# Summing five neighbours in a local attention: one strided reduction or three contiguous additions on VectorE

## The chip, the cores and the metric

One core of a Trainium2 chip. The metric is the device time of one execution of the whole program in microseconds (us), taken over several executions. The kernel is one launch of hand-placed instructions with semaphores between the engines: PE (matmul), DVE (VectorE), ACT (ScalarE), POOL (GpSimd) and SP, whose queue issues nearly all DMAs.

## The reference

The program is a network of three blocks on x of 8 x 128 x 32 x 32, that is eight images of 1024 tokens with 128 channels. What matters here is the middle block. Cut to that:

```python
def _L1_attn_ref(x, ...):                      # per image, 1024 tokens of 128 channels
    x_global = global_mha(x, ..., H_GLOBAL=8)  # full softmax attention
    x_local = local_mha(x, ..., H_LOCAL=4)     # each token and its 5 neighbours
    x_comb = jnp.concatenate([x_global, x_local], axis=-1)
    ...                                        # fused MLP, layer norm, feed-forward, layer norm

def local_mha(x, ...):
    k_win = jnp.stack([kp[:, j:j + Sq] for j in range(WINDOW)], axis=2)
    v_win = jnp.stack([vp[:, j:j + Sq] for j in range(WINDOW)], axis=2)
    scores = jnp.einsum('bshd,bswhd->bshw', q, k_win) / np.sqrt(hd)
    attn = jax.nn.softmax(scores, axis=-1)
    o = jnp.einsum('bshw,bswhd->bshd', attn, v_win).reshape(Bq, Sq, D)
```

Before it stands a convolution-style attention over all tokens of an image ("conv"), and behind it a mixture of eight experts.

## The kernel before, in words

The eight images (called batches 0 to 7) go through a software pipeline, in which three batches are under way at once. A step is a named piece of work of one batch. The steps that matter:

- **conv** of batch a+2: `split_low` stores the parts of its queries and keys, `conv_stacks` (L863, L865, twelve small DMAs) loads them as stacks, `conv_max` (PE L1183, DVE L1666) takes the row maxima of 16 tiles.
- **maxima** of the global attention: per batch two halves (quad 0 and 1) of 64 tiles. `max_tile` is a matmul on PE (L1249) and a reduction on DVE (`gmax`, L1728). `guard` turns the maxima into three bf16 parts, `guard_rows` copies them on DVE (L1743) and SP writes them into the query stack with three DMAs (L898).
- **scores**: `score_tile` (PE L1268, ACT exponential L1523) of a quad can start only when the DMAs of `guard_rows` for that quad have landed. `pv_group` (L1280) is the product with the values.
- `global_stacks` (L891, twelve DMAs of 128 KB) loads the stacks of a quad of the next batch. The first `max_tile` of that quad waits for them.
- **local attention**, four groups g = 0 to 3 of 256 tokens per batch. `local_dot`: SP loads keys and values of the windows into `kv_win` (L908, 1280 KB) and the queries (L909), POOL forms the products `lprod` (L1062). `local_max` on DVE: L1762 sums over the 32 channels of a head, then mask, maximum and subtraction. `local_sum` on DVE (L1778 to L1783) norms, then POOL multiplies with the values (L1069) into `lprod` again. `local_out` on DVE (L1790) sums `lprod` over the five neighbours into `ol_tok`.
- **tail**: the outputs of a batch go through fused MLP, norms and routing, and `store_t2` (L915) writes its tokens.

There is one buffer `kv_win` and one `lprod`. SP's `local_dot` of the next group therefore waits until POOL has finished `local_sum` of the group before, also across batches:

```python
            def local_dot(b, g):
                if not (isinstance(b, int) and b == 0 and g == 0):
                    after(sp, lpv_made, b * 4 + g)
```

Each engine, SP's queue included, runs its own fixed list of steps, in order. These lists are made at build time by `Steps.plan()`, a list scheduler: every step has parts with an engine, a busy time and a latency in the table `PARTS`, and the planner puts next the part that can start first by these numbers, with the longest way to the end breaking ties. The planner knows only the dependences that are given to it. For `local_dot` they are:

```python
        s.add("local", a, ("local_dot", g), (a, ("local_out", g - 1)), (a, ("local_qkv", NT - 2)),
              (a, ("local_qkv", NT - 1)))
```

For g = 0 there is no `local_out` of group -1 in the same batch, so that the wait of `local_dot` 0 for the last group of the batch before is not among them.

## Time and profile before

| what | value |
|---|---|
| median of 3 runs | 1966.23 us (1964.11 to 1969.98) |
| time of the profiled execution | 1971.81 us |
| its span, first to last instruction | 1969.2 us |
| mean granted TensorE clock | 0.888 |
| busy shares PE, DVE, ACT, POOL | 82%, 68%, 52%, 36% |

The batches run until about 1600 us of the span, the rest is the last tail and the eight experts. A busy share is an average over the whole span. A wait names the instruction that released the waiting engine. In the rows of a timeline the first number is the start in us, the second the duration, and what stands in brackets at the end is the idle time just before, with what ended it.

### The profile page before, as it was taken

To read this page: it belongs to the slowest core of one execution; us is meant where nothing else is said; L and a number is where in the kernel's file an instruction comes from. 1 tells how busy PE (TensorE), PEld (TensorE's weight loads), DVE (VectorE), ACT (ScalarE), POOL (GpSimd) and SP (SyncE) were. 2 spreads that over 40 slices of the span, in tenths; PEclk is the share of its full clock that TensorE was granted. 3 is DMA by queue.
4 is the path that set the end of the run, shared out by engine and by line. 5 is a ranking of instruction groups with operands and counts; after the bars stand their busy time and mean duration, and the time that the engine had idled before them with its cause. 6 is when DMAs were issued, how large, how long until landed. Compare 5 with 4: busy or idle time off the path is not lost.

```text
span 1969.2 us, 24543 instructions
## 1 busy us (share of the span) xinstructions
PE 1616.7 (82%) x8264; PEld 759.1 (39%) x8264; DVE 1334.0 (68%) x2698; ACT 1031.5 (52%) x1970; POOL 715.0 (36%) x1113
## 2 busy tenths in 40 slices
PE   5758889998998898979898996889788886339993
PEld 2513322533443253325433442344223322227772
DVE  4258868797789768976897697869698821116660
ACT  1311566477656655665575665656564663223431
POOL 3101301245215530553154315421453441436883
PEclk7765899999999899989998998999898968559995
DMA  5281241335053405241533244132414110023346
GB/s 169 73 152 45 81 102 48 80 128 117 19 125 98 95 13 135 94 95 28 155 95 59 44 141 103 38 44 97 106 66 87 44 38 2 1 81 74 74 55 184
DMA packets 125921, 161.66 MB, mean 82 GB/s; under 512 B 19116, under 2 KB 86449, under 8 KB 125798
## 3 DMA queue, kind: packets, MB, share of 16 engines
q1 hardware_dynamic: 109926, 148.61, 29.6%
q0 software_dynamic: 13568, 7.31, 2.8%
q10 hardware_dynamic: 2304, 4.20, 0.6%
q8 instruction: 65, 1.06, 0.2%
q14 instruction: 58, 0.48, 0.1%
HBM read 103.36 MB, written 58.52 MB: 82 GB/s over the span
## 4 chain that ended last, share of the span: by engine, by line
PE 45%; DVE 18%; POOL 11%; DMA 9%; ACT 7%; SPq 6%; issue 5%; POOLq 0%; DVEq 0%; ACTq 0%
PE bank L1280 8%; PE bank L1249 7%; PE bank L1268 7%; DVE gmax L1728 7%; POOL t_d L1117 6%; PE bank L1206 6%; PE bank L1317 3%; PE bank L1307 3%; PE bank L1127 2%; SPq L891 2%; ACT prob L1523 2%; DVE cmax L1666 2%; DMA k_stack<-parts_d 2%; DMA kv_d<-lqkv 2%; DMA q_stack<-gneg_rows 2%
## 5 line engine op out<-in xcount | busy, mean ns | idle before, releaser
L1523 ACT ACTIVATE prob<-bank 128x512 f32<-128x512 f32 x1024 | 573.4, 596 | 348.8 <-PE bank L1268 346.9
L1728 DVE TENSOR_REDUCE gmax<-bank 128x1 f32<-128x512 f32 x1024 | 653.9, 681 | 65.9 <-PE bank L1249 65.0
L1268 PE MATMUL bank<-q_stack,k_stack 99*128 99x512 bf16 x1024 | 390.4, 397 | 71.1 <-ACT prob L1523 33.8
L1249 PE MATMUL bank<-k_stack,q_stack 96*128 96x512 bf16 x1024 | 402.9, 402 | 55.8 <-DVE gmax L1728 27.5
L1280 PE MATMUL bank<-prob,v_tok 128*32 128x512 f32 x2048 | 282.7, 626 | 2.1 <-ACT prob L1523 2.1
L1062 POOL TENSOR_TENSOR lprod<-ql_tok,kv_win 128x640 f32<-128x640 f32 x64 | 102.2, 1618 | 371.1 <-DMA ql_tok<-ql_d 347.1
L1249 PEld LDWEIGHTS bank<-k_stack,q_stack 96*128 96x128 bf16 x1024 | 101.4, 99 | 316.1 <-DVE gmax L1728 206.3
L1268 PEld LDWEIGHTS bank<-q_stack,k_stack 99*128 99x128 bf16 x1024 | 100.4, 100 | 249.0 <-ACT prob L1523 158.4
L1069 POOL TENSOR_TENSOR lprod<-ls,kv_win 128x640 f32<-128x640 f32 x64 | 80.8, 1284 | 227.5 <-DVE ls L1783 227.1
L1027 POOL TENSOR_TENSOR mv<-stats 128x4 f32<-128x4 f32 x64 | 13.0, 203 | 393.5 <-DVE stats L1700 393.5
L1117 POOL DMA_INDIRECT t_d<-kv_win,token_e x80 | 130.0, 1625 | 53.1 <-DVE kv_win L1928 29.0
L1206 PEld LDWEIGHTS bank<-cv_tok,cprob 128*128 128x128 f32 x960 | 116.3, 195 | 26.8 <-DVE t_tok L1695 12.9
L1206 PE MATMUL bank<-cv_tok,cprob 128*128 128x129 f32 x960 | 124.0, 283 | 1.1 <-DVE t_tok L1695 0.6
L1104 POOL DMA_INDIRECT rows_d<-rows,slot x64 | 63.1, 986 | 135.6 <-DVE slot L1889 118.5
L1666 DVE TENSOR_REDUCE cmax<-bank 128x1 f32<-128x512 f32 x128 | 86.1, 683 | 30.5 <-PE bank L1183 30.0
L1795 DVE SCALAR_TENSOR_TENSOR hid<-tanh_t,half_t 128x512 f32<-128x512 f32 x64 | 53.2, 831 | 52.4 <-ACT half_t L1427 52.2
L1473 ACT ACTIVATE cprob<-bank 128x512 f32<-128x512 f32 x120 | 70.4, 599 | 33.0 <-PE bank L1198 32.4
L1280 PEld LDWEIGHTS bank<-prob,v_tok 128*32 128x32 f32 x2048 | 41.3, 110 | 99.3 <-issue 62.3
L1790 DVE TENSOR_REDUCE ol_tok<-lprod 128x256 f32<-128x1280 f32 x32 | 76.1, 2378 | 0.0
L1691 DVE RECIPROCAL crecip<-bank 128x1 f32<-128x1 f32 x64 | 10.7, 168 | 95.8 <-PE bank L1206 95.6
L1549 ACT ACTIVATE tanh_t<-bank,hcols 128x512 f32<-128x512 f32 x64 | 43.9, 687 | 59.7 <-PE bank L1307 39.3
L1183 PE MATMUL bank<-ck_stack,cq_stack 96*128 96x512 bf16 x128 | 58.7, 467 | 16.1 <-DVE cmax L1666 10.9
(215 smaller groups left out, 2458.3 us busy)
## 6 DMA issues: line engine op xcount, KB each, us to landing
kv_win<-kv_d SPq DMA_DIRECT2D x32, 1280.0 KB, 5.6
parts_d<-parts SPq DMA_DIRECT2D x16, 768.0 KB, 3.6
q_stack<-parts_d SPq DMA_DIRECT2D x96, 128.0 KB, 6.9
k_stack<-parts_d SPq DMA_DIRECT2D x96, 128.0 KB, 7.4
kv_d<-lqkv SPq DMA_DIRECT2D x64, 128.0 KB, 2.5
rows_d<-rows SPq DMA_DIRECT2D x10, 528.0 KB
cprob<-rows_d SPq DMA_DIRECT2D x8, 660.0 KB, 4.7
x_cm<-in_x_dram SPq DMA_DIRECT2D x8, 512.0 KB, 3.5
```

What stands on the lines that cost most here:

```text
L1062: m = pool.tensor_tensor(lprod[:, i, :, :], ql_tok[:, i, None, :].to_broadcast([P, WIN, C]), kv_win[:, i, :, 0:C], ALU.mult)
L1069: m = pool.tensor_tensor(lprod[:, i, :, :].rearrange("p w (h d) -> p w h d", d=LD), ls[:, i, :, :, None].to_broadcast([P, WIN, LH, LD]), k ...
L1117: pool.indirect_dma_start(t2_d, bass.IndirectOffsetOnAxis(ap=token_e[e % 2][:, i:i + 1], axis=0), y_e[e % 2][:, i, :], None, bounds_check= ...
L1206: last = mm(ps[:, 0:C + 1], conv_prob(b, i // HT)[:, j, (i % HT) * P:(i % HT + 1) * P], cv_tok[:, j, :], start=(j == 0), stop=(j == NT - 1))
L1249: mm(max_ps[max_bank(n)][:, :], q_stack[quad][0:KROWS, h, i * P:(i + 1) * P], k_stack[quad][0:KROWS, h, j * HN:(j + 1) * HN], start=True, ...
L1268: mm(score_ps[n % 2][:, :], k_stack[quad][0:KM, h, j * P:(j + 1) * P], q_stack[quad][0:KM, h, half * HN:(half + 1) * HN], start=True, stop ...
L1280: last = mm(o_ps[CG * h:CG * (h + 1), :], v_tok[:, j, quad * QH + h, :], prob[:, g % 2, h, :], start=(j == 0), stop=(j == NT - 1))
L1473: nc.scalar.activation(conv_prob(b, h)[:, j, :], ps[:, :], ACT.Exp).then_inc(free, 1)
L1523: nc.scalar.activation(prob[:, g % 2, h, :], score_ps[n % 2][:, :], ACT.Exp).then_inc(exp_made, 1)
L1666: v.tensor_reduce(cmax[:, t // 2, t % 2:t % 2 + 1], ps[:, :], AX.X, ALU.max)\
L1728: v.tensor_reduce(gmax[:, h, i, j:j + 1], max_ps[max_bank(n)][:, :], AX.X, ALU.max)\
L1790: v.tensor_reduce(ol_tok[:, 2 * g:2 * g + 2, :], lprod[:, :, :, :].rearrange("p i w c -> p i c w"), AX.X, ALU.add).then_inc(ol_made, 1)
```

## The change

`local_out` no longer reduces `lprod` (two token tiles x 5 neighbours x 128 channels per partition) with one TENSOR_REDUCE along a strided axis. It adds neighbours 2 and 3 to neighbours 0 and 1 in place (512 elements per partition), then neighbour 1 to neighbour 0 (256 elements), and last neighbour 4 into `ol_tok` (256 elements). Each addition waits for the one before through a new semaphore `lsum_made`. The planner's busy time for `local_out` goes from 2.3 to 1.5.

```diff
@@ PARTS
-    "local_out": [("dve", 2.3, 0.2)],
+    "local_out": [("dve", 1.5, 0.2)],
@@ semaphores
+        lsum_made = sem("lsum_made")
@@ local_out
                 after(dve, lpv_made, b * 4 + g + 1)
                 if g == 0 and not (isinstance(b, int) and b == 0):
                     after(dve, tail_full, tail_count(b - 1, ("o_channels", 1, 1)) + 1)
-                v.tensor_reduce(ol_tok[:, 2 * g:2 * g + 2, :],
-                                lprod[:, :, :, :].rearrange("p i w c -> p i c w"), AX.X, ALU.add).then_inc(ol_made, 1)
+                v.tensor_tensor(lprod[:, :, 0:2, :], lprod[:, :, 0:2, :], lprod[:, :, 2:4, :], ALU.add)\
+                    .then_inc(lsum_made, 1)
+                after(dve, lsum_made, b * 8 + 2 * g + 1)
+                v.tensor_tensor(lprod[:, :, 0, :], lprod[:, :, 0, :], lprod[:, :, 1, :], ALU.add)\
+                    .then_inc(lsum_made, 1)
+                after(dve, lsum_made, b * 8 + 2 * g + 2)
+                v.tensor_tensor(ol_tok[:, 2 * g:2 * g + 2, :], lprod[:, :, 0, :], lprod[:, :, 4, :], ALU.add)\
+                    .then_inc(ol_made, 1)
```

The one number in the table changes the lists of all engines: over the 667 entries of SP's queue some 40 stand elsewhere, and on PE and DVE hundreds of instructions have traded places. In the changed kernel the lines behind L645 are one higher, so that L898 is L899 there. Three places follow.

The first is SP's queue around the `guard_rows` of batch 5, quad 1. Before, it reads (L908 and L909 at the top are `local_dot` 0 of batch 6, the L891 are `global_stacks` 0 of batch 6, L898 is `guard_rows`, L915 is `store_t2` of batch 4):

```order
L908 DMA kv_win<-kv_d 128x2x1280
L909 DMA ql_tok<-ql_d 128x2x128
L891 DMA q_stack0<-parts_d 16x4x1024
...
L891 DMA k_stack0<-parts_d 16x4x1024
L898 DMA q_stack1<-gneg_rows 1x32x128 x3
L915 DMA t2_d<-x1 128x8x128
```

Now (the first L909 and L910 are `local_dot` 3 of batch 5, the second pair is `local_dot` 0 of batch 6):

```order
L909 DMA kv_win<-kv_d 128x2x1280
L910 DMA ql_tok<-ql_d 128x2x128
L899 DMA q_stack1<-gneg_rows 1x32x128 x3
L892 DMA q_stack0<-parts_d 16x4x1024
...
L892 DMA k_stack0<-parts_d 16x4x1024
L909 DMA kv_win<-kv_d 128x2x1280
L910 DMA ql_tok<-ql_d 128x2x128
```

`guard_rows` has moved ahead of the twelve stack loads and of `local_dot` 0. In batch 3 it has likewise moved ahead of `local_dot` 0 of batch 4, while `global_stacks` has stayed behind it.

The second is DVE around the `guard_rows` copy (L1743) of batch 4, quad 1, with `local_sum` 3 (L1778 to L1783). SP's queue is the same there before and now: `local_dot` 3 of batch 4, `local_dot` 0 of batch 5, `guard_rows`, `global_stacks`. Before:

```order
L1728 TENSOR_REDUCE gmax<-bank1 128x1
L1778 TENSOR_REDUCE lsum<-ls 128x8
L1781 RECIPROCAL lsum<-lsum 128x8
L1783 TENSOR_TENSOR ls<-ls,lsum 128x40
...
L1790 TENSOR_REDUCE ol_tok<-lprod 128x256
L1743 COPY gneg_rows<-bank2 96x128
```

Now:

```order
L1744 COPY gneg_rows<-bank2 96x128
L1802 SCALAR_TENSOR_TENSOR hid<-tanh_t,half_t 128x512
L1667 TENSOR_REDUCE cmax<-bank0 128x1
L1763 TENSOR_REDUCE ls<-lprod 128x40
...
L1779 TENSOR_REDUCE lsum<-ls 128x8
L1782 RECIPROCAL lsum<-lsum 128x8
L1784 TENSOR_TENSOR ls<-ls,lsum 128x40
```

`local_sum` 3 of batch 4, which stood ahead of the copy, now stands behind it. In batch 2 it is the other way round: there `local_sum` 3 stood behind the copy and now stands ahead of it.

The third is SP's queue in batch 2, around the loads of the conv stacks of batch 4. Before (L854 is `split_low` of batch 4, L863 the first of `conv_stacks`):

```order
L854 DMA parts_d<-parts 32x3x1024
L863 DMA cq_stack<-parts_d 16x1024
L865 DMA ck_stack<-parts_d 16x1024
```

Now:

```order
L855 DMA parts_d<-parts 32x3x1024
L909 DMA kv_win<-kv_d 128x2x1280
L910 DMA ql_tok<-ql_d 128x2x128
L864 DMA cq_stack<-parts_d 16x1024
L866 DMA ck_stack<-parts_d 16x1024
```

The pair that has come between is `local_dot` 0 of batch 3.

## Rows read from the trace of the kernel before

**Rows 1.** Page, busy time of each engine
```profile
PE 1616.7 (82%) x8264; PEld 759.1 (39%) x8264; DVE 1334.0 (68%) x2698; ACT 1031.5 (52%) x1970; POOL 715.0 (36%) x1113
```

**Rows 2.** Page, the chain that ended last, by engine
```profile
PE 45%; DVE 18%; POOL 11%; DMA 9%; ACT 7%; SPq 6%; issue 5%; POOLq 0%; DVEq 0%; ACTq 0%
```

**Rows 3.** Stretches: length, busy PE, PEld, DVE, ACT, POOL, then clock, DMA share, GB/s
```profile
950.00:1000.00 50.00, 47.14 (x215) 18.89 (x214) 47.63 (x81) 34.40 (x66) 20.22 (x31) 0.97 0.38 123
1200.00:1250.00 50.00, 31.12 (x156) 13.46 (x154) 32.74 (x67) 19.38 (x37) 16.47 (x28) 0.80 0.39 69
```

**Rows 4.** DVE groups by shape: busy us, mean ns, idle before
```profile
L1790 DVE TENSOR_REDUCE ol_tok<-lprod 128x256 f32<-128x1280 f32 x32 | 76.1, 2378 | 0.0
L1795 DVE SCALAR_TENSOR_TENSOR hid<-tanh_t,half_t 128x512 f32<-128x512 f32 x64 | 53.2, 831 | 52.4 <-ACT half_t L1427 52.2
L1918 DVE TENSOR_TENSOR kv_win<-kv_win,prob_e 128x512 f32<-128x512 f32 x16 | 11.1, 692 | 0.5
L1783 DVE TENSOR_TENSOR ls<-ls,lsum 128x40 f32<-128x40 f32 x32 | 8.7, 271 | 1.1
L1918 DVE TENSOR_TENSOR kv_win<-kv_win,prob_e 128x256 f32<-128x256 f32 x8 | 3.4, 425 | 0.3
```

**Rows 5.** One line's instructions: ns min/median/max, of L1795 and of L1762
```profile
L1795 DVE SCALAR_TENSOR_TENSOR hid<-tanh_t,half_t x64: 672/682/1919, 375.4 to 1704.5; 128x512 f32<-128x512 f32 x64
L1762 DVE TENSOR_REDUCE ls<-lprod x32: 1462/1476/1487, 151.0 to 1562.8; 128x40 f32<-128x1280 f32 x32
```

**Rows 6.** Waits of PE for the guard rows: us in total, times, longest
```profile
PE bank L1268 <- DMA q_stack<-gneg_rows: 32.6, 4, 14.8
```

**Rows 7.** Timeline of DVE, POOL, SP and PE at the turn of batch 3
```profile
833.88 0.21 DVE L1743 COPY gneg_rows<-bank 96x128 bf16<-96x128 bf16 x1
839.80 2.48 POOL L1069 TENSOR_TENSOR lprod<-ls,kv_win 128x640 f32<-128x640 f32 x2 [11.92 <-DVE ls L1783]
843.23 1.95 SPq L898 DMA_DIRECT2D q_stack<-gneg_rows  x3
850.55 1.01 PE L1268 MATMUL bank<-q_stack,k_stack 99*128 99x512 bf16 x2 [9.65 <-DMA q_stack<-gneg_rows]
864.10 0.67 DVE L1728 TENSOR_REDUCE gmax<-bank 128x1 f32<-128x512 f32 x1
```

**Rows 8.** The same at the turn of batch 4
```profile
1020.72 0.20 DVE L1783 TENSOR_TENSOR ls<-ls,lsum 128x40 f32<-128x40 f32 x1
1028.91 0.20 DVE L1743 COPY gneg_rows<-bank 96x128 bf16<-96x128 bf16 x1
1048.63 0.68 DVE L1728 TENSOR_REDUCE gmax<-bank 128x1 f32<-128x512 f32 x1
```

**Rows 9.** The same at the turn of batch 5
```profile
1213.77 0.21 DVE L1743 COPY gneg_rows<-bank 96x128 bf16<-96x128 bf16 x1
1235.64 1.01 PE L1268 MATMUL bank<-q_stack,k_stack 99*128 99x512 bf16 x2 [14.85 <-DMA q_stack<-gneg_rows]
1237.12 0.69 DVE L1728 TENSOR_REDUCE gmax<-bank 128x1 f32<-128x512 f32 x1 [7.73 <-PE bank L1249]
```

**Rows 10.** Batch 2: the conv stacks, and the turn
```profile
619.20 0.33 SPq L863 DMA_DIRECT2D cq_stack<-parts_d  x1
625.22 0.36 SPq L837 DMA_DIRECT2D x_cm<-in_x_dram  x1
632.48 0.69 DVE L1666 TENSOR_REDUCE cmax<-bank 128x1 f32<-128x512 f32 x1
641.16 0.21 DVE L1743 COPY gneg_rows<-bank 96x128 bf16<-96x128 bf16 x1
656.65 1.01 PE L1268 MATMUL bank<-q_stack,k_stack 99*128 99x512 bf16 x2 [5.83 <-DMA q_stack<-gneg_rows]
670.84 0.68 DVE L1728 TENSOR_REDUCE gmax<-bank 128x1 f32<-128x512 f32 x1
```

**Rows 11.** DMA issues of the conv stacks: KB each, us to landing
```profile
ck_stack<-parts_d SPq DMA_DIRECT2D x48, 32.0 KB, 1.8
```

## Prediction

> **What bounds the kernel now.** I read the busy shares first, then the chain, then the stretches, and last the waits and the timeline around them. Over the span PE is busy 1616.7 us and DVE 1334.0 us [rows 1], and the chain that ended last lies on PE for 45% and on DVE for 18% [rows 2]. Neither share says what DVE time is worth. The stretches do. While maxima are taken, PE and DVE are both nearly full: 47.14 and 47.63 us of 50 [rows 3]. There a microsecond of DVE is worth part of a microsecond, since PE has under 3 us of slack in 50. In other stretches both are idle together, as from 1200 to 1250 us, with 31.12 and 32.74 us of 50 and the clock down at 0.80 [rows 3]. So something else holds both, and the waits name it: PE stands 32.6 us, in four waits, for the DMA of the guard rows [rows 6].
>
> The turn of batch 3 shows where they come from [rows 7]. DVE has the guard rows ready at 834.1 us. SP issues them only at 843.23, because ahead of them in its queue stands the window load of the next batch's `local_dot` 0, and that waits for POOL's product, which ends at 842.28. Its two issues fill the time to 843.23. PE goes idle, and starts the scores after 9.65 us. The first maxima of batch 4 come at 864.10, which is 30.2 us after the guard rows. At the turn of batch 4 the order on DVE was kinder: its `local_sum` 3 was done at 1020.9, before the guard rows at 1028.91, so that SP's queue was free, and the next maxima came 19.7 us later [rows 8]. Those two, 30.2 and 19.7, are a bad turn and a good one. Batch 2 is a bad one too (641.16 to 670.84, 29.7 us, PE idle for 5.83) [rows 10], and batch 5 has the longest stall, 14.85 us, since the guard rows stood behind the twelve stack loads as well, though its maxima came after 23.3 us [rows 9].
>
> **The additions themselves.** Removed are 32 reductions of 2378 ns, 76.1 us of DVE [rows 4]. Added are 32 times one addition of 512 and two of 256 elements per partition. The nearest rows are products of two SBUF operands in that shape, 692 and 425 ns [rows 4]: 692 + 2 x 425 = 1542 ns. Two waits of an instruction for the one before it cost 1.1 us / 32 = 34 ns each (L1783) [rows 4]. That gives 1.61 us, the low bound. The high bound comes from L1795, which also reads two SBUF tiles of 512 elements: its median is 682 ns but its mean 831 and its longest 1919, while a reduction that reads one tile stays between 1462 and 1487 [rows 4, 5]. If the additions are stretched as on average there, 0.149 us per 512 elements, their 1024 elements cost 0.30 us more: 1.91 us. I take the high one, since `lprod` is of just this kind, and get a saving of 2.38 - 1.91 = 0.47 us x 32 = 15 us of DVE (25 us at the low bound).
>
> The Trainium skill, on the page "SBUF — State Buffer" (section "Who interferes with whom"), speaks against this part of the change: `tensor_tensor` with both inputs in SBUF reads through an interface shared with GpSimd and contends with GpSimd's reads, while `tensor_reduce` never does. By that rule the trace agrees: 682 against 1919 ns for L1795, no spread for L1762. Without the rule one would sum with 1.61 us and save 25 us of DVE, with it 15.
>
> How much of the 15 us shows in the time? By my count in stretches of 50 us, 19 of the 32 reductions lie in maxima-bound ones like 950 to 1000 [rows 3], the others beside PE-bound work, where they are hidden and stay so even if they cost more. 19 x 0.47 = 9 us, and PE has slack for about half. I take **-4 us**, between 0 and -15 (19 x 0.77).
>
> **What the new order moves.** The change is also a change of the lists, and by the rows above this is the larger part. Turn by turn:
>
> - Batch 5, quad 1: guard rows now ahead of stacks and `local_dot` 0, and behind only `local_dot` 3, whose release (`local_sum` 2) stands ahead on DVE. The 14.85 us of idle PE [rows 9] can go in full, with some 2 us of slow clock after it. But the first maxima of batch 6 need the stack loads, and can come at best 19.7 instead of 23.3 us after the guard rows. Between -3.6 and -16.9, I take the middle, **-10 us**.
> - Batch 3: guard rows ahead of `local_dot` 0, so the 9.65 us go. The stack loads stay behind `local_dot` 0, and start 2 us earlier at best (the three guard issues, 1.95 us, are gone from between) [rows 7]. PE gets its scores early and is then short of maxima. Between -2 and -12.9 (9.65 and some 3 us of slow clock, 850 to 858 us), I take **-5 us**.
> - Batch 2: `local_sum` 3 moves ahead of the guard rows on DVE, which makes a bad turn a good one: 29.7 - 19.7 = -10 us [rows 8, 10]. Against that stands the third place of the order. The conv stacks of batch 4 now queue behind `local_dot` 0 of batch 3, which waits for DVE's `local_sum` 3. The fifteen steps from `split_low` to its end on DVE are nine `gmax` and two `cv_tok` at 0.6, two of the tail at 0.6, `local_max` 2.1 and `local_sum` 0.7 (the planner's own busy times, near the rows): 10.6 us. With POOL's 2.5 and SP's 0.9 [rows 7], and `split_low` done some 2.4 us ahead of the first stack load, the stacks start at 619.2 - 2.4 + 14.0 = 630.8 us instead of 619.20. Twelve issues take 5.7 us, the landing 1.8 [rows 10, 11]. They are there at 638.3, where the first `cmax` stood at 632.48 [rows 10]: **+6 us**, with PE behind it in order. Sum of the batch **-4 us**.
> - Batch 4: the reverse. `local_sum` 3 moves behind the guard rows on DVE, while SP still has `local_dot` 0 of batch 5 ahead of them. A good turn becomes a bad one: 30.2 - 19.7 = **+10 us** [rows 7, 8], up to +13 if it stalls the scores as in batch 5.
>
> The other turns keep a guard that is issued at once. `keep` has moved ahead of `global_stacks` 1 in batches 3 and 4, which costs its two issues of 0.4 us, because ACT's norm has moved ahead of the last score tile too. The tail of batch 0 has moved forward, so that `store_t2` stands ahead of the conv stacks of batch 3: about free if that tail is on time. I cost these at nothing, with 8 us either way for what I cannot see. The experts, from about 1640 us on, are untouched.
>
> **Sum.** -4 - 10 - 5 - 4 + 10 = -13 us on the profiled execution of 1971.8 us, which lies 5.6 us above the median. From the median of 1966.2 that is **1953 us**. Differences under 0.3%, 6 us, can't be told from none here.
>
> **The rivals.**
>
> 1. *The stalls were all there was.* PE is full elsewhere, so each lost stall counts in full: -16.9, -12.9 and -10 for batches 5, 3 and 2, +10 for batch 4, -4 for DVE: -34 us, 1932 us. For it: clock and both engines sag together in rows 3. Against: the stack loads keep the pace of the maxima. Chance 0.2.
> 2. *Nothing to see.* The planner trades stalls one for one, and only the -4 us of DVE stay: 1962 us. For it: batches 2, 3 and 4 as costed above already sum to +1, and only batch 5 stands out. Chance 0.2.
> 3. *Slower, by SP's queue.* `local_dot` 0 is planned as if it waited for nothing, and everything behind it stands. If batch 4 pays +13, the conv stacks of batch 4 pay +6 with a cold PE behind (+3), batch 5 gives back only 3.6, batch 3 only 2, batch 2's turn only its 5.83, the DVE term is 0 and some of the unseen 8 us goes the wrong way, the sum is +11 to +19: about 1980 us. It decides from the point where the two new waits cost PE over 16 us together. Chance 0.19.
> 4. *The additions don't save.* If POOL were reading during all of them, at the longest of L1795 (1919 for 682 ns, 2.8 times), they would take 4.3 us against 2.38. POOL is busy 36% of the span [rows 1], and under that share the mean of L1795 is what gave 1.91 us above. To cost DVE time on the whole, half of the additions would have to meet POOL, some +10 us. By the page named above this is the way in which the change would be slower. Chance 0.03, time 1976 us.
>
> **How the numbers follow.** The forecast, -6 to -25 us, has 0.38; rival 1 0.2; rival 2 0.2; rivals 3 and 4 0.22. Faster by over 0.3% is 0.58, within 0.3% 0.2, slower 0.22. The range leaves out the far ends of rivals 1 and 3: 1930 to 1977 us. The forecast's own range is 1941 to 1960.
>
> **What would show it.** In the profile of the changed kernel: three groups in place of L1790, near 830, 500 and 500 ns with a spread in their maxima, 1.9 us together; PE's wait for the guard rows once and not four times, at the turn of batch 4, near 10 us; none of over 3 us at the turns of batches 2, 3 and 5; a new wait of PE or DVE for `ck_stack` of about 6 us in batch 2; and a wait for `k_stack` at the first maxima of batch 4. The prediction is wrong if the guard-row stalls are still there in batches 3 and 5, if the turn of batch 4 stays near 20 us, or if the time moves by more than the turns do, which would point to PE's and DVE's own order.

## The result: 1.5% slower, and the profile after

The kernel after took 1996.91 us (median of 4 runs, 1990.17 to 2002.73), the kernel before 1966.23 us. The ratio is 1.0152, with a 95% interval of 1.0111 to 1.0194. The forecast was 1953 us, so it had the wrong sign. The profiled execution took 1990.17 us, against 1971.81 before. The median of before moves between 1966 and 1988 us from one set of runs to another, so everything below is given as a ratio to the kernel before, timed beside it in the same set. The traces are of single executions from these sets, so that a stretch of one set held against a stretch of another can be off by the same 1%. The traced pair of before and after differs by 18.4 us, the medians by 30.7. Three executions of the kernel before in the slow state (5134.93, 7463.07 and 8167.00 us) are left out.

The first part of the page of the kernel after, and of its chain:

```profile
span 1987.6 us, 24607 instructions
...
PE 1632.7 (82%) x8264; PEld 760.3 (38%) x8264; DVE 1320.2 (66%) x2762; ACT 1031.6 (52%) x1970; POOL 723.3 (36%) x1113
...
PE 45%; DVE 18%; POOL 11%; DMA 8%; ACT 7%; SPq 5%; issue 5%; POOLq 0%; DVEq 0%; ACTq 0%
```

DVE is busy for 13.8 us less than in [rows 1]. PE executes the same 8264 matmuls, but is busy 16.0 us longer. Its idle time hardly moved: 1987.6 - 1632.7 = 354.9 us, and 1969.2 - 1616.7 = 352.5 before. So most of the loss in this pair of executions stands in longer matmuls, at a mean granted clock of 0.881 in place of 0.888.

The groups of the new additions and of L1802, the L1795 of before, by line (busy us, mean ns of one, then the idle time before them):

```profile
L1802 DVE SCALAR_TENSOR_TENSOR hid<-tanh_t,half_t 128x512 f32<-128x512 f32 x64 | 50.2, 785 | 57.5 <-ACT half_t L1428 57.3
L1791 DVE TENSOR_TENSOR lprod<-lprod 128x512 f32<-128x512 f32 x32 | 23.2, 724 | 3.4 <-POOL lprod L1070 3.1 <-PE bank L1128 0.2
L1794 DVE TENSOR_TENSOR lprod<-lprod 128x256 f32<-128x256 f32 x32 | 16.5, 515 | 1.1
L1797 DVE TENSOR_TENSOR ol_tok<-lprod 128x256 f32<-128x256 f32 x32 | 15.5, 485 | 1.1
```

A set takes 0.724 + 0.515 + 0.485 + 0.069 = 1.79 us, between the bounds of 1.61 and 1.91. Against 76.1 us [rows 4] the three groups have 55.2.

PE's waits after (total us, times, longest), beside [rows 6]:

```profile
PE bank L1269 <- ACT prob L1524: 38.9, 62, 3.5
PE bank L1250 <- DMA k_stack<-parts_d: 35.0, 8, 16.3
...
PE bank L1269 <- DMA q_stack<-gneg_rows: 12.3, 3, 4.5
PE bank L1184 <- DMA ck_stack<-parts_d: 11.9, 2, 8.4
```

The named stalls did go: the wait for the guard rows fell from 32.6 to 12.3 us (4.49 at the turn of batch 4, 3.41 and 4.39 at quad 0 of batches 6 and 7). Others grew in its place: for `k_stack` from 27.0 to 35.0, for `ck_stack` to 11.9.

Where the time went is seen from one mark per batch, the start of the guard-row copy of quad 1 on DVE (L1743, L1744 after). There the maxima of a quad end and its guard rows go out; the expectations below call it a shift. The turn of a batch is the time from this mark to the first global maxima of the next batch. The two columns on the right are experiments told below, and all numbers are us from the start of each span.

| batch | before | after | additions, old order | strided sum, new order |
|---|---|---|---|---|
| 1 | 459.6 | 449.0 | 456.5 | 457.1 |
| 2 | 641.2 | 664.0 | 640.3 | 672.2 |
| 3 | 833.9 | 853.2 | 832.3 | 862.5 |
| 4 | 1028.9 | 1049.4 | 1029.5 | 1061.2 |
| 5 | 1213.8 | 1240.3 | 1217.4 | 1252.5 |
| 6 | 1398.0 | 1419.1 | 1401.8 | 1430.7 |
| 7 | 1559.9 | 1584.8 | 1569.1 | 1595.2 |
| span | 1969.2 | 1987.6 | 1970.6 | 1996.0 |

At the mark of batch 1 the kernel after is ahead by 10.6 us. From there to the mark of batch 2 it takes 215.0 us where before took 181.6, and loses 33.4. After that it gains and loses a few us per batch. With quad 0 of batch 2 as a mark between (555.7 before, 562.3 after), the first half of this loss, 17 us, belongs to the turn of batch 1, on which the prediction put nothing. The second half, 16 us, is batch 2. Of the 33.4 us, 10.6 only use up the lead: at the next mark the kernel after is 22.8 us behind.

SP's queue at the turn of batch 1, first before (L854 is `split_low` of batch 3, L863 and L865 the conv stacks, L898 the guard rows, L891 the global stacks):

```profile
451.35 0.32 SPq L854 DMA_DIRECT2D parts_d<-parts  x1
453.68 0.34 SPq L863 DMA_DIRECT2D cq_stack<-parts_d  x1
...
459.80 1.78 SPq L898 DMA_DIRECT2D q_stack<-gneg_rows  x3
461.69 0.52 SPq L891 DMA_DIRECT2D q_stack<-parts_d  x1
```

And after (L909 is `local_dot` 0 of batch 2, L916 `store_t2` of batch 0):

```profile
449.20 1.78 SPq L899 DMA_DIRECT2D q_stack<-gneg_rows  x3
451.14 0.47 SPq L909 DMA_DIRECT2D kv_win<-kv_d  x1
...
459.46 0.32 SPq L855 DMA_DIRECT2D parts_d<-parts  x1
463.29 0.38 SPq L916 DMA_DIRECT2D t_d<-x  x1
463.77 0.52 SPq L864 DMA_DIRECT2D cq_stack<-parts_d  x1
...
471.04 0.36 SPq L892 DMA_DIRECT2D q_stack<-parts_d  x1
```

The guard rows are issued at once in both. But the conv stacks of batch 3 now stand behind them, and the global stacks of batch 2 behind those, 21.8 us after the guard rows in place of 1.9. The last of these stacks lands at 485.87 us and the next global maxima come at once, 37.4 us after the guard-row copy (before: landed at 477.53, maxima 18.8 us after the copy). From the first maxima to the copy of quad 0 it is 75.9 us, and 77.3 before. So the whole 17 us lie in when the global stacks are there.

SP's queue alone doesn't explain when that is. `global_stacks` overwrites what `score_tile` reads, so it also waits for PE's last score tile of the same quad of the batch before. These are the last two of quad 0 of batch 1, before and then after:

```profile
460.31 0.60 PE L1268 MATMUL bank<-q_stack,k_stack 99*128 99x512 bf16 x2
...
465.71 0.60 PE L1269 MATMUL bank<-q_stack,k_stack 99*128 99x512 bf16 x2
```

They end 1.3 us behind the copy before, and 17.3 us behind it after. So two things hold the stacks after, each by itself: PE's order until 17.3 us, and SP's queue until 22.1. In SP's queue `split_low` stands ahead, which waits for DVE's `parts` (L1656) until 459.45, and then the conv stacks. A change of SP's queue alone could win 4.8 us at most, and one of PE's order alone nothing. In PE's order 13 score tiles of quad 0 follow its last maximum of quad 1, where 8 did, and together with parts of the conv projection of batch 3 they take 20.8 us where 10.5 were enough.

The stretches 450 to 500, 650 to 700 and 850 to 900 us, before and then after (length, busy us of PE, PEld, DVE, ACT, POOL, granted clock, DMA share, GB/s):

```profile
450.00:500.00 50.00, 44.18 (x246) 17.82 (x244) 37.97 (x88) 35.47 (x72) 24.16 (x54) 0.97 0.46 87
...
650.00:700.00 50.00, 42.30 (x228) 19.37 (x220) 32.32 (x73) 31.13 (x64) 23.99 (x54) 0.86 0.43 91
...
850.00:900.00 50.00, 46.25 (x264) 21.93 (x264) 36.81 (x85) 33.92 (x69) 25.62 (x64) 0.93 0.32 57
```

```profile
450.00:500.00 50.00, 39.65 (x190) 14.99 (x189) 27.00 (x52) 30.82 (x63) 23.39 (x45) 0.83 0.52 115
...
650.00:700.00 50.00, 40.88 (x178) 11.93 (x178) 35.16 (x77) 31.93 (x65) 24.06 (x54) 0.81 0.41 76
850.00:900.00 50.00, 34.66 (x156) 11.85 (x156) 30.77 (x68) 23.66 (x49) 21.85 (x35) 0.80 0.34 61
```

In the first of them PE runs 190 matmuls in place of 246, and its granted clock is 0.83 in place of 0.97. There is no long stall in it to name, the longest is 3.54 us. It is many short waits, and a granted clock of 0.83 means that part of the time was spent at 1.2 GHz.

### The profile page after: what moved, and what is told of

The parts are those of the page before. It is cut to its first block, busy times and chain, and to the rows that moved or that the text cites. A ratio compares the mean times of both kernels' runs of the same rounds, so it can differ in the third digit from the quotient of the medians.

```text
span 1987.6 us, 24607 instructions
## 1 busy us (share of the span) xinstructions
PE 1632.7 (82%) x8264; PEld 760.3 (38%) x8264; DVE 1320.2 (66%) x2762; ACT 1031.6 (52%) x1970; POOL 723.3 (36%) x1113
## 4 chain that ended last, share of the span: by engine, by line
PE 45%; DVE 18%; POOL 11%; DMA 8%; ACT 7%; SPq 5%; issue 5%; POOLq 0%; DVEq 0%; ACTq 0%
PE bank L1281 8%; PE bank L1250 8%; PE bank L1269 7%; DVE gmax L1729 7%; POOL t_d L1118 6%; PE bank L1207 6%; DMA k_stack<-parts_d 4%; PE bank L1318 3%; PE bank L1128 3%; PE bank L1308 3%; ACT prob L1524 3%; SPq L892 3%; DVE cmax L1667 2%; PE bank L1199 2%; PE bank L1226 1%
## 5 line engine op out<-in xcount | busy, mean ns | idle before, releaser
L1250 PE MATMUL bank<-k_stack,q_stack 96*128 96x512 bf16 x1024 | 412.0, 409 | 65.0 <-DMA k_stack<-parts_d 35.0
L1269 PE MATMUL bank<-q_stack,k_stack 99*128 99x512 bf16 x1024 | 395.9, 403 | 56.4 <-ACT prob L1524 38.9
L1281 PE MATMUL bank<-prob,v_tok 128*32 128x512 f32 x2048 | 287.7, 636 | 1.3 <-ACT prob L1524 1.2
L1207 PEld LDWEIGHTS bank<-cv_tok,cprob 128*128 128x128 f32 x960 | 115.6, 194 | 24.1 <-DVE t_tok L1696 11.9
L1802 DVE SCALAR_TENSOR_TENSOR hid<-tanh_t,half_t 128x512 f32<-128x512 f32 x64 | 50.2, 785 | 57.5 <-ACT half_t L1428 57.3
L1184 PE MATMUL bank<-ck_stack,cq_stack 96*128 96x512 bf16 x128 | 59.7, 474 | 26.8 <-DVE cmax L1667 14.3
L1037 POOL TENSOR_TENSOR rstd<-mv,half_pow 128x4 f32<-128x4 f32 x64 | 64.9, 1014 | 5.0
```

Of the source, the lines that this page charges most:

```text
L1037: step(tt(scale, m[:, 1, :], half_pow[:, :], ALU.pow))
L1207: last = mm(ps[:, 0:C + 1], conv_prob(b, i // HT)[:, j, (i % HT) * P:(i % HT + 1) * P], cv_tok[:, j, :], start=(j == 0), stop=(j == NT - 1))
L1250: mm(max_ps[max_bank(n)][:, :], q_stack[quad][0:KROWS, h, i * P:(i + 1) * P], k_stack[quad][0:KROWS, h, j * HN:(j + 1) * HN], start=True, ...
L1269: mm(score_ps[n % 2][:, :], k_stack[quad][0:KM, h, j * P:(j + 1) * P], q_stack[quad][0:KM, h, half * HN:(half + 1) * HN], start=True, stop ...
L1281: last = mm(o_ps[CG * h:CG * (h + 1), :], v_tok[:, j, quad * QH + h, :], prob[:, g % 2, h, :], start=(j == 0), stop=(j == NT - 1))
```

## The experiments

### Order and additions apart

The first run (e1) undoes the number in the table and keeps the additions. The second (e2) is the kernel before with 1.5 in place of 2.3.

```diff
-    "local_out": [("dve", 1.5, 0.2)],
+    "local_out": [("dve", 2.3, 0.2)],
```

> The three additions as in the change, the planner's entry for `local_out` back at 2.3, so every engine keeps the order of the kernel before. Theory A (the loss is all in the new order of steps): the additions give back only what DVE's critical work saves, so 1956 to 1966 us against 1966 before, a ratio of 0.995 to 1.000, and TensorE's busy time stays near the 1617 us of before. Theory B (the additions themselves lose, by disturbing POOL and ACT or by shifting when transfers start): near 1985 to 1997, ratio above 1.008, POOL's instructions longer than before. The DVE group of the sum should read 724, 515 and 485 ns under either.

> The strided reduction of the kernel before, with the planner's entry at 1.5, so every engine has the changed kernel's order. Theory A (order alone): slower than the changed kernel by the 4 to 15 us that the additions spare, so 2000 to 2012 us, ratio about 1.02 to 1.025. Theory B (the additions lose): back near 1966, ratio 0.997 to 1.003. The first large gap to the kernel before should open at the turn of batch 1 under A (a guard-row shift near 460 us and the next batch's shift near 575 us or later).

Measured: e1 1.0045 (1.0028 to 1.0061), e2 1.0147 (1.0129 to 1.0165). The new order alone makes the loss of the kernel after, and the table above shows it lost in the same place, from batch 1 to batch 2 (+33.5 us against before). That part of theory A holds. Its range for e2, 1.02 to 1.025, was missed, because the additions spare no time in that order. And neither theory had the rest: the additions, in an order that is otherwise untouched, cost 0.45%.

### Single placements in SP's queue

A loop behind the planner moves a step in SP's list alone. In e3:

```diff
         orders = all_steps()
+        for late, behind in [((0, ('store_t2',)), (4, ('load_x',)))]:
+            orders["sp"].remove(late)
+            orders["sp"].insert(orders["sp"].index(behind) + 1, late)
```

> The changed kernel, with one step moved in SP's queue: the store of batch 0's second tail, which stood between `split_low` and `conv_stacks` of batch 3 at the turn of batch 1, comes behind the convolution's and the global stacks of that turn, as in the kernel before. Theory A1 (this step, costed at nothing in the prediction, holds the stacks and makes the 17 us lost at batch 1's turn): 1975 to 1985 us, ratio against before 1.005 to 1.010, and the gap between batch 1's second shift and batch 2's first closes from 113 us to near 98. Theory A2 (the loss at that turn comes from `local_dot` 0 and `split_low` of batch 3 standing behind the guard rows, on SP and in the order of the other engines): no difference beyond 3 us, 1992 to 2000.

Measured: 1.0088 (1.0071 to 1.0105). The time is in A1's range, but the mark it named moved little: from batch 1's quad 1 to batch 2's quad 0 the trace shows 110.7 us, for 113.3 after and 96.1 before. The global stacks went out 18.4 us behind the copy in place of 22.1, and the next maxima came 36.2 us behind it in place of 37.4. PE's last score tile of quad 0 ended at 16.2, so that little more was to be had there. The time is clear of e2's, which has the order of the kernel after and was timed in the same set (1.0129 to 1.0165).

The same loop was used with other pairs from here on. Its first use on `local_dot` 0 in the changed kernel, with that of batches 3, 4 and 5 behind the first global stacks of the same batch, has no time: with that order the waits close a circle, and the kernel can't run. e7 moves `local_dot` 0 of batch 3 behind `conv_stacks` of batch 4, and e11 does this and the move of e3.

> The changed kernel with `local_dot` 0 of batch 3 in SP's queue behind `conv_stacks` of batch 4 in place of ahead of it: one held group of stacks is taken away. Theory A3 (the 8.4 us wait for ck_stack at 652 us is a cause): it goes, and the changed kernel gains 6 to 12 us, ratio to the kernel before 1.005 to 1.012. Theory A4 (given back in the same turn): within 3 us of the changed kernel, ratio 1.012 to 1.018.

> The changed kernel with two steps moved in SP's queue: batch 0's `store_t2` behind the loads of batch 4 (alone: 1.0088) and batch 3's `local_dot` 0 behind `conv_stacks` of batch 4 (alone: 1.0083), against 1.0152 for the changed kernel. Theory A (the two losses stand at different turns and add up): 1.000 to 1.004, which leaves nearly none of the order's loss. Theory E (a later turn takes back what these give): 1.006 to 1.010.

Measured: e7 1.0083 (1.0052 to 1.0115), e11 1.0056 (1.0038 to 1.0073). In e7 the 8.4 us wait is gone, and so are 12.5 us between the two shifts of batch 2 (89.2 us for 101.7). Both runs are faster than the kernel after, e3 clear of its interval and e7 within a hair of it, and e11 more so. Whether the two gains (0.64% and 0.69%) add up can't be told from e11's 0.96%, given the intervals. E is nearer than A, and the trace shows something of it, within the 1% between sets: e11 reaches the mark of batch 3 at 839.2 us, 14 ahead of the kernel after, and that of batch 4 at 1044.3, 5 ahead. The stretch from batch 1's to batch 2's shift stays at 113.0 us. Its stacks went out at 18.4 us behind the copy, with PE's last score tile of quad 0 at 16.2: the part that PE's order holds is untouched. Other orders that came up agree. Where that last score tile comes early, 4.1 us behind the copy in e14 (below) and 4.7 in e12, the conv stacks stand ahead of the guard rows as well and the stretch takes 98.6 and 98.2 us. In e6 the tile ends 13.0 us behind the copy, SP's queue has been free since 8.3, the stacks go out at 13.1 and the stretch takes 107.7. No run moved that tile alone, so that its price is read from these traces and not measured by itself.

### Is a named stall worth its time?

The prediction's premise was tested on the kernel before, strided sum and all, with only `local_dot` 0 of batches 3, 4 and 6 moved behind the guard rows (e4), or further, behind the global stacks of their own batch (e8). e5 and e9 are the same with additions.

> The kernel before with one edit in SP's queue and nothing else: `local_dot` 0 of batches 3, 4 and 6 comes directly behind `guard_rows` 1 of the batch before, ahead of which it stood, so the second shift's rows no longer queue behind a wait for the last `local_out` (8.2, 9.3 and 8.3 us of queueing in the trace of before). Theory B1, the prediction's premise (a named wait of PE that goes turns into time): TensorE's waits of 5.8, 9.7 and 14.9 us go and the kernel takes 1940 to 1955 us, ratio 0.987 to 0.994. Theory B2 (the waits stand beside other shortages at the turn, and what is saved there is lost within the same turn): ratio 0.997 to 1.003, with the first maxima of the next batch still 19 to 30 us behind the rows.

> The additions with the planner's entry at 2.3 (the order of the kernel before) and the same edit of SP's queue as in the run before this one: a version that could beat both kernels. Theory B1: about 8 us above the kernel before for the additions in the old order (1.0045 measured) less the 12 to 25 us of the edit, so ratio 0.990 to 0.998. Theory B2: 1.002 to 1.007, as the additions alone.

Measured: e4 0.9998 (0.9976 to 1.0020), e5 1.0043 (1.0022 to 1.0063). Three stalls of 5.8, 9.7 and 14.9 us went, and not a microsecond came of it. PE's waits in e4:

```profile
PE bank L1252 <- DMA k_stack<-parts_d: 38.6, 8, 15.4
...
PE bank L1186 <- DVE cmax L1669: 25.3, 18, 7.6
...
PE bank L1271 <- DMA q_stack<-gneg_rows: 5.7, 2, 4.4
```

The wait for the guard rows is down from 32.6 to 5.7 us, and those for `k_stack` and the conv maxima are up from 27.0 and 10.9 to 38.6 and 25.3: 26.9 us gone, 26.0 come. At the turn of batch 3 the 9.65 us at the scores [rows 7] have become this, 9.6 us later:

```profile
860.10 0.59 PE L1252 MATMUL bank<-k_stack,q_stack 96*128 96x512 bf16 x1 [11.12 <-DMA k_stack<-parts_d]
```

I took the stack loads, which still stood behind `local_dot` 0, for what bound the turn. e8 lets them go first:

> The kernel before with `local_dot` 0 of batches 3, 4 and 6 moved in SP's queue behind `global_stacks` 0 of the same batch, one step further than behind the rows, where the edit was worth nothing (0.9998). Theory D1 (the turn ends at the first global maxima of the next batch, and these wait for the k_stack transfers, which stand behind the same wait for the last `local_out`): now the stacks are issued 2.7 us behind the rows at turns 2 and 3 in place of 8.7 to 9.9, the first maxima come 19 to 21 us behind them in place of 28 to 29, and two turns give 6 to 9 us each: 0.991 to 0.996. Theory D2 (the stacks' data or TensorE's other work bind anyway, or the products now late starve the batch later): 0.997 to 1.003.

> The additions with the planner's entry at 2.3 and the same edit as in the run before this one: the candidate to beat both kernels. D1: the additions' 1.004 less 12 to 18 us, 0.995 to 1.000, and less than the strided reduction with the same edit by nothing that can be measured. D2: 1.002 to 1.007.

Measured: e8 1.0052 (1.0031 to 1.0072), e9 1.0095 (1.0068 to 1.0121). Both theories fall, it is slower. The timeline of batch 2's turn in e8 shows why, on POOL, DVE and PE (start, duration, and in brackets the idle time before):

```profile
666.50 3.02 POOL L1065 TENSOR_TENSOR lprod<-ql_tok,kv_win 128x640 f32<-128x640 f32 x2 [18.36 <-DMA ql_tok<-ql_d]
...
669.56 1.49 DVE L1765 TENSOR_REDUCE ls<-lprod 128x40 f32<-128x1280 f32 x1 [16.88 <-POOL lprod L1065]
...
672.43 0.61 PE L1186 MATMUL bank<-ck_stack,cq_stack 96*128 96x512 bf16 x1 [18.78 <-DVE cmax L1669]
```

`local_dot` 0 is no neutral load that holds up others. POOL's product needs it, DVE's list has the maximum over that product (L1765) ahead of the next conv and global maxima, and DVE stands there for 16.88 us with all of them queued behind. The window's loads were issued 5.2 us later than before (653.71 us for 648.48), and POOL started 12.8 us behind them, now beside the stack loads, in place of 7.1. The stacks had landed 22.1 us behind the copy, and the first maxima came 40.3 us behind it (26.4 and 29.7 before). So the stacks and the local window both have to be early, and whichever is late holds the turn.

> The changed kernel (its own order, entry 1.5) with five steps moved in SP's queue alone: batch 0's `store_t2` behind the loads of batch 4; `local_dot` 0 of batches 2, 4 and 5 behind the first global stacks of the same batch; that of batch 3 behind the rows of batch 2. Theory A (the loss is SP's queue at these turns, and the orders of the other engines cost nothing): 1.000 to 1.005, level with the additions in the old order. Theory E (the other engines' orders, PE's and DVE's, carry the rest, as the lower granted clock does): 1.006 to 1.010, no better than moving `store_t2` alone (1.0088) or `local_dot` alone (1.0083).

Measured: 1.0302 (1.0276 to 1.0328), twice the loss that it should mend, and outside both theories. PE now waits 23.10 us at 493 us and 19.85 at 1115, each just after DVE's L1766 had waited 23.9 and 19.4 us for POOL's product: the mechanism of e8, in the new order. So e10 could not decide between its theories.

### Does a truer number in the table help?

> The kernel before, instruction for instruction, with the planner's entry for `local_out` at 2.2 in place of 2.3: nothing that is computed changes, and the entry is as true as before. Theory C1 (what moves the time is how near the entry is to the real cost, 1.91 us with its share of idle): a move of 0.1 gives ratio 0.998 to 1.002. Theory C2 (any other entry gives another draw of the order at eight turns, each worth up to 17 us): the order differs at four turns and the ratio lies anywhere from 0.99 to 1.02, most likely above 1.004.

> The strided sum everywhere, with the planner's entry at 2.0. If the additions are worth their DVE time in an order that keeps them clear of POOL, this is 5 to 12 us slower than e14's 1.0007: 1.003 to 1.007. If DVE's time is worth nothing there, the same as e14: 0.999 to 1.002.

> The additions with the planner's entry at 1.8, which is what a set really takes (724 + 515 + 485 ns and some 0.07 us between them). Theory C1 (a true entry gives a good order): 0.995 to 1.002, below the additions in the old order (1.0045). Theory C2 (each entry is another draw): 1.004 to 1.018.

> The additions with the planner's entry at 2.0, between the true cost and the old entry. Theory C1: 0.998 to 1.003. Theory C2: 1.004 to 1.018, in no relation to the distance from 1.79 us.

| entry for `local_out` | strided sum | additions |
|---|---|---|
| 2.3 | 1 (the kernel before) | 1.0045 (1.0028 to 1.0061), e1 |
| 2.2 | 1.0074 (1.0045 to 1.0103), e6 | |
| 2.0 | 1.0030 (1.0009 to 1.0051), e18 | 1.0007 (0.9990 to 1.0023), e14 |
| 1.8 | | 1.0029 (1.0012 to 1.0046), e12 |
| 1.5 | 1.0147 (1.0129 to 1.0165), e2 | 1.0152 (1.0111 to 1.0194), after |

The left column computes the same with the same instructions. A change of the entry by 0.1 costs 0.7%, one by 0.3 less than half of that. C2 is right in that near the true cost the time doesn't follow the distance, but its range for e12 and e14 (1.004 to 1.018) was missed by both: e14 lies in C1's range and e12 between the two. The entry 1.5 is the slowest in both columns, so a far entry may still be worse than a near one. With the strided sum, which takes 2.38 us, the entry 2.3 is the best of four. With additions the true entry, 1.8, is no better than 2.0, whose interval overlaps with its own. At 2.0 the additions may be worth a little: 1.0007 for 1.0030, with intervals that overlap. The two were timed in different sets, and e17 below, with additions in 30 of the 32 sets and timed together with e18, reads 1.0022.

### Why do the additions lose in the old order?

A set means the three additions, or the one strided sum, of one group of one batch; there are 32.

Three pairs agree on 0.45%: e1 and before, e5 and e4 (1.0043 and 0.9998), e9 and e8 (1.0095 and 1.0052). First (e13) I tried to give the set its old length back.

```diff
+                v.tensor_tensor(lprod[:, :, 1, :], lprod[:, :, 1, :], lprod[:, :, 4, :], ALU.add)\
+                    .then_inc(lsum_made, 1)
+                after(dve, lsum_made, b * 12 + 3 * g + 3)
```

> The additions in the old order (entry 2.3, alone 1.0045) with a fourth addition of 256 elements between the second and the third, which only overwrites a column that nothing reads again: the set is again about 2.3 us long, as the strided sum was, and the form (several instructions with waits between them) stays. Theory P (the loss comes from the shorter set, which shifts DVE's maxima against TensorE's scores): 0.998 to 1.002. Theory Q (it comes from the form, waits between instructions or their traffic to SBUF beside POOL): 1.004 to 1.009.

Measured: 1.0083 (1.0062 to 1.0104). The run does not separate the two: it lies in Q's range, but its set is 2.57 us on average, longer than the strided sum, so that P wasn't put to the test. The reason for that length is that the additions' lengths fall into two classes. Two lines of e1, with the shortest, median and longest duration in ns:

```profile
L1791 DVE TENSOR_TENSOR lprod<-lprod x32: 675/680/1522, 175.6 to 1578.7; 128x512 f32<-128x512 f32 x32
...
L1794 DVE TENSOR_TENSOR lprod<-lprod x32: 424/425/1383, 176.3 to 1579.4; 128x256 f32<-128x256 f32 x32
```

Of the 32 sets of e1, 26 take 1.6 us and six take 4.0 to 4.3, which makes 2.07 on average. In e13 26 take 2.1 us and the same six 4.1 to 5.4. One of the six in the timeline, on DVE and then on POOL:

```profile
815.85 1.43 DVE L1791 TENSOR_TENSOR lprod<-lprod 128x512 f32<-128x512 f32 x1
817.31 1.37 DVE L1794 TENSOR_TENSOR lprod<-lprod 128x256 f32<-128x256 f32 x1
818.72 1.37 DVE L1797 TENSOR_TENSOR ol_tok<-lprod 128x256 f32<-128x256 f32 x1
...
815.46 1.27 POOL L1084 TENSOR_TENSOR x<-x,bc 128x512 f32<-128x512 f32 x1
816.81 1.59 POOL L1086 TENSOR_TENSOR x<-x,bc 128x512 f32<-128x512 f32 x1
818.48 1.33 POOL L1090 TENSOR_TENSOR a_old<-x,bc 128x512 f32<-128x512 f32 x1
```

Each addition lasts about as long as one POOL instruction beside it. The same place in the kernel before:

```profile
817.91 2.43 DVE L1790 TENSOR_REDUCE ol_tok<-lprod 128x256 f32<-128x1280 f32 x1
...
817.52 1.27 POOL L1083 TENSOR_TENSOR x<-x,bc 128x512 f32<-128x512 f32 x1
818.87 1.27 POOL L1085 TENSOR_TENSOR x<-x,bc 128x512 f32<-128x512 f32 x1
820.22 1.27 POOL L1089 TENSOR_TENSOR a_old<-x,bc 128x512 f32<-128x512 f32 x1
```

The strided sum takes 2.43 us there, and 2.32 to 2.42 where POOL is idle. And this is e1's next matmul for a global maximum, which waited for the DVE reduction behind the three additions:

```profile
820.75 0.39 PE L1250 MATMUL bank<-k_stack,q_stack 96*128 96x512 bf16 x1 [1.33 <-DVE gmax L1729]
```

Two runs put the additions only in the 26 clear sets (e15), and only in the six (e16), by the number of the set. This is e15; e16 has both conditions the other way round:

```diff
+                lsums = 2 * sum(n not in (7, 14, 18, 22, 26, 30) for n in range(b * 4 + g))
+                if not ((b * 4 + g) not in (7, 14, 18, 22, 26, 30)):
+                    v.tensor_reduce(ol_tok[:, 2 * g:2 * g + 2, :],
+                                    lprod[:, :, :, :].rearrange("p i w c -> p i c w"), AX.X, ALU.add).then_inc(ol_made, 1)
+                else:
...
```

> The old order (entry 2.3), with the strided sum kept in the six sets that ran beside POOL's bias additions (batch 1 set 3; batches 3 to 7 set 2) and the additions in the other 26. Theory R (the loss of the additions is the stretch of those six, 4.1 us in place of 2.4, which are late in the turn): the 26 sets spare 26 x 0.78 = 20 us of DVE, none is stretched, and the time is at or below that of before, 0.994 to 1.000. Theory Q (the form costs, wherever it stands): 1.002 to 1.005, as with additions everywhere (1.0045).

> The old order, with additions in those six sets alone and the strided sum in the other 26. Theory R: six sets are 1.6 to 1.9 us longer each, some 10 us of DVE, at places where TensorE waits for the maxima: 1.003 to 1.007. Theory Q: six sets of 32 carry a fifth of the cost, 0.999 to 1.002.

Measured: e15 0.9983 (0.9958 to 1.0007), e16 1.0045 (1.0026 to 1.0065). Six sets alone bring the whole loss of the additions, and the other 26 bring none. The groups of e16:

```profile
L1793 DVE TENSOR_REDUCE ol_tok<-lprod 128x256 f32<-128x1280 f32 x26 | 61.7, 2374 | 0.0
...
L1799 DVE TENSOR_TENSOR lprod<-lprod 128x256 f32<-128x256 f32 x6 | 8.3, 1375 | 0.2
L1802 DVE TENSOR_TENSOR ol_tok<-lprod 128x256 f32<-128x256 f32 x6 | 8.2, 1373 | 0.2
L1796 DVE TENSOR_TENSOR lprod<-lprod 128x512 f32<-128x512 f32 x6 | 7.5, 1253 | 0.0
```

The six are 1.6 us longer each than the strided sum, 10 us together, and cost 0.0045 x 1984 = 9 us: nearly a full microsecond for each. The 26 spare 26 x 0.78 = 20 us of DVE, and 3 us of that show, with an interval that includes none. PE's waits for `gmax`, in total 27.5 us before, are 38.1 in e16, 31.3 in e1 and 26.7 in e15. Summed over the 8 us from the start of each of the six sets, PE waits for `gmax` 0.7 us before, 7.9 in e1, 7.8 in e16 and 0.5 in e15: most of the 9 us stand right there. Behind the other 26 sets it waits for `gmax` only 2.2 us before, so there was little to win. Longer POOL instructions are no rival of that size: its three lines of such additions (L1084, L1086 and L1090 in e16) take 2.5 us more in all than before. By the same price e13 fits too: its six sets take 14.5 us more than six strided sums, which is 0.7%, inside its interval.

> The additions with the planner's entry at 2.0 (alone: 1.0007), with the strided sum kept in the two sets that ran beside POOL there (batches 6 and 7, set 2). Theory R: two stretches of 1.8 to 2.2 us go, so 0.998 to 1.001, the best of the versions so far. Theory Q: 1.0005 as before, no difference.

Measured: 1.0022 (0.9997 to 1.0048), no gain over e14's 1.0007 that can be told. The two sets it spares stand in batches 6 and 7. No version here beats the kernel before beyond its interval; e15 comes nearest.

## Why the prediction was wrong, point by point

From mark to mark the terms compare like this (us, after less before). The prediction's -4 us for the additions belong to no stretch, and the traced pair shows 18.4 of the 30.7 us between the medians.

| stretch, from mark to mark | forecast | measured |
|---|---|---|
| start to batch 1 | 0 | -10.6 |
| batch 1 to quad 0 of batch 2 | 0 | +17.2 |
| quad 0 of batch 2 to batch 2 | +6 | +16.2 |
| batch 2 to 3 | -10 | -3.5 |
| batch 3 to 4 | -5 | +1.2 |
| batch 4 to 5 | +10 | +6.0 |
| batch 5 to 6 | -10 | -5.4 |
| batch 6 to the end | 0 | -2.7 |

- **Costed at nothing: batch 1.** This is the largest step that failed. The prediction saw `store_t2` ahead of the conv stacks of batch 3, called it "about free if that tail is on time", and put nothing on this turn, with 8 us either way for all that it could not see. It cost 17 us. The guard rows themselves went out at once, but the global stacks of batch 2 were issued 22.1 us behind the copy in place of 2.1. They were held twice: in SP's queue behind `split_low` and the conv stacks of batch 3, and by PE's last score tile of quad 0, which ended at 17.3 us in place of 1.3. The prediction looked at neither, and the store that it did look at was worth 3.7 us of the stacks' delay (e3). The prediction's own sign for this, a time that "moves by more than the turns do", came true.
- **Stalls as time.** The sum rested on turning named waits into microseconds. e4 took away three of them for nothing. The prediction named the successor ("PE gets its scores early and is then short of maxima") and priced it too low.
- **Batch 2, -4 us.** That the conv stacks would be held was right: `split_low` was issued at 628.93 us and the first stack at 644.3, 15.4 us later where I had worked out 14.0, and PE stood 8.4 us where +6 was put. The price was wrong: the stretch around it grew by 16.2 us, and e7, which undoes this one placement, is faster by 0.69%, 14 us. The turn itself gave 29.7 - 25.4 = 4.3 us and not 10.
- **The additions, -4 us.** The set was sized rightly for the new order (1.79 us, bounds 1.61 and 1.91), and its worst case too: rival 4 worked out 4.3 us, and 4.0 to 4.3 were seen. In the old order the mean is 2.07 us, above the high bound. The step that failed was to spread the stretch evenly and multiply a mean by a mean price. In the old order the sets' price is +9 us where POOL works and -3 elsewhere (e16, e15), the latter not clear of nothing. In the new order three sets of 32 were stretched, and the additions are worth nothing that can be measured (1.0152 and 1.0147). Rival 4 asked for half of the sets to meet POOL. By its own figures (1.6 us clear, 4.3 beside POOL, 2.38 for the strided sum) some nine sets would have been enough to cost DVE time. In fact six of 32 made the kernel slower while DVE still saved time, since PE was waiting for the maxima behind those six and hardly behind the others. By the Trainium skill's "SBUF — State Buffer" (section "Who interferes with whom"), which the prediction cited, a `tensor_tensor` with both inputs in SBUF contends with GpSimd's reads and a `tensor_reduce` does not. The rows agree: 1.37 us for 0.42, and 2.43 for 2.38.
- **Turn of batch 5, -10 us.** The stall went, and the maxima came 19.2 us after the copy, as said. From the mark of batch 5 to that of batch 6 it is 178.8 us for 184.2, so -5.4: inside the bounds (-3.6 to -16.9), and half of the middle that I took.
- **Turn of batch 3, -5 us.** The stall went, but the stack loads went out 14.3 us behind the copy in place of 11.4, where the prediction had them earlier by 2 us. The maxima came 35.8 us after the copy in place of 30.2, and the stretch to the next mark is 196.2 us for 195.0.
- **Turn of batch 4, +10 us.** The maxima came 37.1 us after the copy for 19.7, with a stall of 4.49 at the scores where 10 was expected, and +6.0 us to the next mark (190.9 for 184.9). The sign was right and the size a bit large.
- **The clock.** PE's busy time grew by 16 us, which was not in the sum beyond a few us at single stalls. The lower granted clock stands in the thinner stretches such as 450 to 500 us; no run took the clock apart from the order.

Rival 3 had the direction but not the size: it put the kernel at 1980 us, and 1996.9 is 17 us above that and 20 above the top of the range. Its mechanism, SP's queue at batches 2 and 4, was there, but the largest loss was at batch 1, where PE's order held the stacks too.

## What to carry to other kernels

A wait in an in-order pipeline is worth its time only if what stands next in all the other lists is early too; take the wait away by itself first (as e4 does), before pricing an order by its stalls. When a load is late, look at both things that it waits for, its place in the queue and the last reader of its buffer. When an edit changes a planner's number, time the new order with the old instructions and the new instructions in the old order, since here the number was worth 1.5% and the instructions 0.5%. And an average cost hides collisions: find where two-input DVE instructions meet POOL, and price those few places apart.

## What the runs showed of the hardware that I had not expected

An addition of 256 elements on DVE with both inputs in SBUF took 0.42 us alone and 1.37 us while POOL ran additions of 1.27 us, so that in these sets DVE went forward at POOL's pace, one instruction for one. POOL paid little: its 1.27 us became 1.59 for the one in the middle, the mean of its L1086 1510 ns (1336 before), while that of L1084 fell from 1453 to 1412. And part of the loss at the turns is not idle time but a lower clock: between before and after PE's idle time differs by 2.4 us and its busy time, for the same matmuls, by 16.0 (granted clock 0.888 and 0.881). In e2, with the same order as after, it is about half and half: 1629.6 us busy and 366.4 idle, 12.9 and 13.9 above before, at 0.887.
